# A fused attention, mixer and expert kernel: the mixer's normalisations on ScalarE, its first statistics in the attention loop, biases in the weights, ranks summed on TensorE, four pipeline stages in another order

## What is computed

```python
x = x + agent_attention(group_norm(x))          # masked attention over the 16 agents, 5 masks
t = x.reshape(32, 512, 128)
n = ln(t)                                       # (v - mean) / sqrt(var + 1e-5), per token
q, k, v = elu(n @ Wq + bq) + 1, elu(n @ Wk + bk) + 1, n @ Wv + bv      # 8 heads of 16
t = t + q @ (k.T @ v) / (q @ k.sum(tokens))     # linear attention, per sample and head
n = ln(t)
logits = n @ router_w + router_b                # 8 experts; the best two, softmax over the two
t = t + sum over the two experts of share * expert(n)
```

## Time and profile before

| | |
|---|---|
| median of 3 runs | 1396.28 us (1394.41 to 1402.51) |
| the profiled execution | 1391.66 us, span of its trace 1389.8 us |
| mean granted PE clock | 0.889 of 2.4 GHz |
| busy share of the span | PE 81%, DVE 70%, ACT 47%, POOL 41% |
| HBM | 33.47 MB read, 24.72 MB written, 42 GB/s over the span |

### The profile page before, as it was taken

How to read it: one execution, slowest core, us unless ns; L and a number is a source line. 1 busy time by engine, 2 the same in 40 slices (tenths; PEclk the granted TensorE clock), 3 DMA queues, 4 the chain that set the end, 5 groups by cost and what they waited for, 6 DMA issues and landing times. The chain is left out here.

```text
span 1389.8 us, 39348 instructions
## 1 busy us (share of the span) xinstructions
PE 1127.9 (81%) x12771; PEld 888.4 (64%) x12772; DVE 966.2 (70%) x2723; ACT 653.5 (47%) x1221; POOL 574.5 (41%) x575
## 2 busy tenths in 40 slices
PE   4599999999749978767777841099999999999995
PEld 4377877777615565546455541088888888887884
DVE  5476666766436887887878777077777777777774
ACT  0276665666214432232332310166666666666663
POOL 0335556555611133453354445234444444444443
PEclk9899999999959877777878765599999999999997
DMA  7010101010030001111111113911111111111100
GB/s 269 18 46 26 33 25 34 25 33 10 3 108 16 16 15 49 32 45 48 32 39 50 37 60 75 124 46 50 43 51 50 47 49 43 48 51 50 37 20 1
DMA packets 72632, 64.40 MB, mean 46 GB/s; under 512 B 10098, under 2 KB 58512, under 8 KB 72522
## 3 DMA queue, kind: packets, MB, share of 16 engines
q1 hardware_dynamic: 58698, 43.91, 11.5%
q0 software_dynamic: 10016, 17.16, 4.0%
q10 hardware_dynamic: 3808, 1.91, 1.1%
HBM read 33.47 MB, written 24.72 MB: 42 GB/s over the span
## 5 line engine op out<-in xcount | busy, mean ns | idle before, releaser
L1295 PE MATMUL e_ps<-e_xt,w_hl 128*128 128x256 f16 x736 | 202.1, 275 | 18.6 <-issue 16.0
L1247 POOL DMA_INDIRECT out<-e_y,e_xg x184 | 182.0, 989 | 78.9 <-issue 78.9
L1372 DVE SCALAR_TENSOR_TENSOR e_hid_hl<-e_hid,e_hid_hl 128x512 f16<-128x512 f32 x184 | 127.4, 693 | 108.7 <-ACT e_hid_hl L1345 96.1
L1296 PE MATMUL e_ps<-e_xt,w_hl 128*128 128x256 f16 x736 | 201.3, 274 | 0.0
L1297 PE MATMUL e_ps<-e_xt,w_hl 128*128 128x256 f16 x736 | 201.2, 273 | 0.0
L1345 ACT ACTIVATE e_hid_hl<-e_hid 128x512 f16<-128x512 f32 x184 | 115.9, 630 | 143.9 <-DVE e_hid L1366 82.3
L756 POOL TENSOR_TENSOR m_stw<-m_stw,m_half 128x8 f32<-128x8 f32 x32 | 53.6, 1682 | 263.8 <-DVE m_stw L1015 263.8
L1312 PE MATMUL e_ps<-w_hl,e_hid_hl 128*128 x736 | 153.9, 223 | 0.0
L1311 PE MATMUL e_ps<-w_hl,e_hid_hl 128*128 x736 | 152.5, 223 | 0.0
L768 POOL DMA_INDIRECT rows<-m_rows,m_place x128 | 130.9, 1023 | 50.4 <-issue 40.5
L1313 PE MATMUL e_ps<-w_hl,e_hid_hl 128*128 x736 | 151.4, 220 | 0.0
(11 more groups left out here) (241 smaller groups left out, 2759.9 us busy)
## 6 DMA issues: line engine op xcount, KB each, us to landing
e_xg<-rows SPq DMA_DIRECT2D x92, 133.0 KB
resid<-in_x SPq DMA_DIRECT2D x8, 1024.0 KB, 12.5
xb<-in_x SPq DMA_DIRECT2D x32, 256.0 KB, 2.6
m_rows<-resid SPq DMA_DIRECT2D x32, 256.0 KB, 2.7
out<-e_y,e_xg POOLq DMA_INDIRECT x184
m_w_f<-in_L_ffn_gate_up_proj SPq DMA_DIRECT2D x1, 2048.0 KB, 8.8
rows<-m_rows,m_place POOLq DMA_INDIRECT x128
rows<-nobody SPq DMA_DIRECT2D x15, 133.0 KB
```

The lines of the kernel that those rows point to most:

```text
L1247: nc.gpsimd.indirect_dma_start(out_rows, bass.IndirectOffsetOnAxis(ap=who, axis=0), y[:, slot, i, :], None, bounds_check=B * TOK - 1, oob_ ...
L1295: t.matmul(o, hi, x2[0], start=True, stop=False)
L1296: t.matmul(o, hi, x2[1], start=False, stop=False)
L1372: v.scalar_tensor_tensor(hid_hl[:, i, 1].rearrange("p q n -> p (q n)"), hid[:, i], 1.0 / (WS * QG), hid_hl[:, i, 0].rearrange("p q n -> p ...
```

## The change

- **Normalisations on ACT.** Both `norm` stages become 128x128 activations (Identity with scale and bias from a tile). POOL makes scale and bias: after the pow it also multiplies mean and factor, and adds the constant `lift`, all in the small tiles. The words rstd, shift and token number are written by ACT (`meta`).
- **First statistics in the attention loop.** The eight bn_stats per pair are DVE instructions of block 1 (`statistics`, one body behind `add`). In the mixer the six small instructions run once over all pairs, and POOL raises 8, then 16, then 104 columns.
- **Biases in the weights.** Wq, Wk, Wv and the router are one tile `wall`. (bias + 1 for q and k) is spread over the 128 rows of the weights and the mean of the columns taken out (`wall`, once), with LIFT making the transposed input carry the constant. So the bias matmuls, the bias operand of the exp, and the bias addition in `route` go. exp takes a bias of -1, and max(min(exp, 1), q) read from PSUM replaces relu and addition; the Relu passes go.
- **Ranks on PE.** The one-hot is f16; 18 small matmuls per pair add region base, earlier counts, earlier partitions and earlier tokens of the same partition. `sum16`, `same`, `earlier`, `spot` go from DVE. The ranks read a DVE result that stands after the whole of `route`.
- **Four bodies deep instead of six**, another order on every engine, `route` and statistics no longer woven. Folds go four experts per body in bodies 0 and 1; the weights' splits in three parts of 3, 3 and 2 experts, the last `weights_low` after the table.
- **Loads.** Constants, weights and biases of the mixer are loaded by SP at the end of the attention's second pass.

The diff, cut to its core ("..." marks what is left out):

```diff
@@ agent_attention
+            for tile, source in mixer["loads"]:
+                sp.dma_start(tile, source).then_inc(mixer["loads_in"], 16)
...
+            def statistics(k, ring, u):
+                e = 2 * k + u
+                ...
+                for j in range(TILES):
+                    v.bn_stats(mixer["st1"][:, e, j, :], resid[:, e, j * C:(j + 1) * C])
...
-                (3, add, 0), (1, reciprocals), (3, add, 1),
+                (4, statistics, 0), (4, statistics, 1), (3, add, 0), (1, reciprocals), (3, add, 1),
             ])
+            for u in range(2):
+                statistics(PAIRS - 1, 0, u)
@@ token_mixer, gpsimd
+            def power(k, ring):
+                w = stw[:, ring]
+                pool.wait_ge(s.stat2, LN_STEPS * (k + 1))
+                ...
+                g.tensor_tensor(w[:, 5, :], w[:, 4, :], half[:, 0:8], ALU.pow).then_inc(s.pow2, 1)
+                g.tensor_tensor(w[:, 6, :], w[:, 3, :], w[:, 5, :], ALU.mult).then_inc(s.pow2, 1)
+                g.tensor_tensor(w[:, 5:7, :], w[:, 5:7, :], ..., ALU.add).then_inc(s.pow2, 1)
...
+            pipelined(pool, PAIRS, 4, 2, [
+                (0, ring_power), (3, rows_ready), (3, send, 0), (3, send, 1), (0, biases_low), (1, power),
@@ token_mixer, scalar
+            def norm2(k, ring, u):
+                b = 2 * k + u
+                need(act, s.pow2, 3 * k + 3)
+                need(act, s.xT2, b - 1)
+                for j in range(TILES):
+                    i = u * TILES + j
+                    ins = a.activation(xn2[:, u, j * C:(j + 1) * C], resid[:, b, j * C:(j + 1) * C], ACT.Identity,
+                                       scale=stw[:, ring, 5, i:i + 1], bias=stw[:, ring, 6, i:i + 1])
+                ins.then_inc(s.norm2, 1)
...
+            pipelined(act, PAIRS, 4, 2, [
+                (0, norm1, 0), (2, norm2, 0), (0, xt_, 0), (0, norm1, 1), (0, queries, 0), (2, xt2_, 0), (2, norm2, 1), (0, xt_, 1),
+                (0, values, 0), (2, xt2_, 1), (0, keys, 0), (0, queries, 1), (2, meta), (0, keys, 1), (2, ew), (0, values, 1),
+                (0, weights), (0, biases),
@@ token_mixer, tensor
+            t.matmul(bank_s[:, 0:WALL], minus64[:], wall[:], start=True, stop=False)
+            t.matmul(bank_s[:, 0:WALL], plus64[:], wrow[:], start=False, stop=True).then_inc(s.wall_psum, 1)
...
-                    t.matmul(banks_kv[:, n], ones16[0:64, :], bkv_hl[:].rearrange("p i c -> p (i c)"), start=True, stop=False)
...
             def ranks(k, ring):
+                need(pe, s.route, ROUTE_STEPS * k + ROUTE_STEPS)
+                need(pe, s.place_done, k)
+                t.matmul(rank, part16[:], each(base16[:], 8), start=True, stop=False)
+                t.matmul(rank, ones16[:], each(ahead16[:], 8), start=False, stop=False)
+                for n in range(7):
+                    t.matmul(rank[:, (n + 1) * G:8 * G], ones16[:], each(oh16[:, n, :], 7 - n), start=False, stop=False)
+                t.matmul(rank, before16[:], oh16[:].rearrange("p n g -> p (n g)"), start=False, stop=True)
+                for n in range(8):
+                    last = t.matmul(seen, ident16[:], oh16[:, n, :], start=n == 0, stop=n == 7)
...
+            pipelined(pe, PAIRS, 4, 2, [
+                (1, sums, 0), (0, xT, 0), (1, outs, 0), (1, sums, 1), (0, q, 0), (2, xT2, 0), (1, outs, 1), (0, xT, 1), (0, k_v, 0),
+                (2, xT2, 1), (2, logits, 0), (2, logits, 1), (0, q, 1), (0, k_v, 1), (0, fold), (2, ranks),
@@ token_mixer, vector
+            small(chain(dve, s.stat1, 0), st1[:].rearrange("p b j n -> p (b j) n"), stw1[:])
+            v.scalar_tensor_tensor(wall[:], wall[:], 2.0, bank_s[:, 0:WALL], ALU.mult, ALU.add).then_inc(s.wall_done, 1)
...
+            def queries(k, ring, u):
+                ...
+                v.scalar_tensor_tensor(qf[:, u, :], ef[:, u, 0, :], 1.0, bank_q, ALU.min, ALU.max).then_inc(s.qf_done, 1)
...
             def keys_values(k, ring, u):
-                v.tensor_tensor(kv[:, u, 0:C], bank_s[:, 0:C], const(cst, "block_kv"), ALU.mult)
-                v.tensor_tensor(kv[:, u, C:C + H], bank_s[:, C:C + 1].to_broadcast([P, H]), const(cst, "block_ks"), ALU.mult).then_inc(s.kv_done, 1)
+                v.tensor_tensor(kv[:, u, :], bank_s[:, 0:C + H], const(cst, "block_kv"), ALU.mult).then_inc(s.kv_done, 1)
...
+            def placed(k, ring):
+                need(dve, s.rank_psum, k + 1)
+                step(v.tensor_tensor(picked[:], oh16[:], rank.rearrange("p (n g) -> p n g", g=G), ALU.mult))
+                step(v.tensor_reduce(best[:, 10, :], picked[:], AX.X, ALU.add))
+                step(v.tensor_copy(place[:, slot:slot + 2, :], w3(best[:, 10, :])), False)
+                v.tensor_tensor(ahead16[:], ahead16[:], seen, ALU.add).then_inc(s.place_done, 1)
...
+            pipelined(dve, PAIRS, 4, 2, [
+                (1, keys_values, 0), (1, mixed, 0), (1, keys_values, 1), (1, statistics, 0), (1, mixed, 1), (0, queries, 0), (1, statistics, 1),
+                (1, second_stats), (0, keys, 0), (2, route), (0, queries, 1), (2, shares), (2, placed), (0, keys, 1),
+                (0, folded), (0, weights_early),
```

More of the change, by code:

```diff
@@ L43 @@
 ROW = C + 5
[L44 removed]
+LN_STEPS, ROUTE_STEPS, EXP_STEP, PLACE_STEPS, COLUMN_STEP = 7, 14, 9, 10, 26
+WALL = 3 * C + E
 LIFT = 0.5
@@ L78, in _constants @@
     put(1, "region", np.tile(np.arange(G) * float(REGION), (P, 1)))
-    put(1, "earlier", np.tile((np.arange(8)[:, None] > np.arange(8)[None, :]).reshape(-1) * 1.0, (P, 1)))
+    put(1, "lift", np.concatenate([np.zeros((P, 8)), np.full((P, 8), LIFT)], 1))
     packed = np.array([E * a + b for a, b in PAIRS_OF] + [1])
@@ L927, in fold @@
                 pe.wait_ge(s.b_in, 32)
-                for e in range(2 * k, 2 * k + 2):
+                for e in range(4 * k, 4 * k + 4):
                     need(pe, s.fold_done, e)
@@ new lines, in statistics, with second_stats @@
+            def statistics(k, ring, u):
+                b = 2 * k + u
+                if isinstance(b, int):
+                    dve.wait_ge(s.add_done, b + 1)
+                for j in range(TILES):
+                    ins = v.bn_stats(st6[:, u * TILES + j, :], resid[:, b, j * C:(j + 1) * C])
+                if u:
+                    ins.then_inc(s.stat2, 1)
+            def second_stats(k, ring):
+                need(dve, s.stat2, LN_STEPS * k + 1)
+                need(dve, s.norm2, 2 * k - 2)
+                need(dve, s.meta_done, k - 1)
+                small(chain(dve, s.stat2, LN_STEPS * k + 1), st6[:], stw[:, ring])
@@ L1086, in route @@
-                pair = const(cst, "pair_code").rearrange("p (o g) -> p o g", o=1).to_broadcast([P, 8, G])
-                yield from step(v.tensor_tensor(oh[:], wide(best[:, 8, :], G), pair, ALU.is_equal), False)
-                other = best[:, 8:9, :].to_broadcast([P, 8, 8])
-                yield from step(v.tensor_tensor(same[:], wide(best[:, 8, :], 8), other, ALU.is_equal))
-                with nc.allow_low_precision(reason="counts up to 8"):
-                    counts = v.tensor_reduce(sum16[:], oh[:].rearrange("p n g -> p g n"), AX.X, ALU.add)
@@ L1092, in route @@
-                yield from step(counts, False)
-                yield from step(v.tensor_tensor(same[:], same[:], const(cst, "earlier").rearrange("p (n m) -> p n m", n=8), ALU.mult))
-                yield from step(v.tensor_reduce(best[:, 10, :], same[:], AX.X, ALU.add), False)
-            def placed(k, ring):
-                d, slot = 2 * k, 2 * ring
+                found3 = logit.rearrange("p (n e) -> p n e", e=E)
+                step(v.tensor_reduce(best[:, 0, :], found3, AX.X, ALU.max))
@@ L1125, in placed @@
-                need(dve, s.place_done, k + 1)
-            pipelined(dve, PAIRS, 6, 2, [
-                (2, keys_values, 0), (1, norm, 0, 0, xn, s.pow1, s.norm1), (4, norm, 0, 1, xn2, s.pow2, s.norm2),
-                (1, norm, 1, 0, xn, s.pow1, s.norm1), (4, norm, 1, 1, xn2, s.pow2, s.norm2), (2, keys_values, 1),
-                (2, mixed, 0), (3, mixed_ready), [(4, route), (0, stats, 0, s.stat1), (3, stats, 1, s.stat2)], (4, placed),
-                (1, feature, 0), (2, mixed, 1), (5, weights_low), (1, feature, 1), (0, folded),
+                step(v.tensor_tensor(rows[:, slot:slot + 2, :, WLO], w3(two), w3(more), ALU.add), False)
```

386 lines of the change are left out of this document (195 added, 191 removed).

## The result

The changed kernel took 1356.66 us (median of 4 runs, 1352.62 to 1364.09) against 1395.35 for the kernel before: a ratio of 0.9736, 95% interval 0.9695 to 0.9776. Faster, by 39 us; 1269 was forecast, and the range ended at 1312. The profiled execution took 1352.62 us, its span is 1350.8.

What follows compares the result with a forecast made beforehand. DVE's queue, the fullest, plus hand-offs bound the mixer. Early bodies to 481, twelve of 18.5 to 703, last place 731, plus 37: experts at 768 instead of 895.4, 127 less; 1264.5 profiled, 4.6 more for the median: 1269 us, range 1245 to 1312.

Steps and rivals of the forecast that it cites:

- idle time of the steady body: Mixer's looped body: DVE's loop turn 0.9, hand-offs 1.6 and low clock 0.5 us, added to 15.4 of work.
- `mixed` 1 meets `outs` 1: Steady mixer body: DVE reaches this product and waits some 0.4 us for PE's result.
- POOL 13, under cover: Steady mixer body: POOL's sends 10.4 us, one pow 1.65 and four tiny instructions sum to 13, fitting under 18.5.
- body 18.1: Steady mixer body: forecast about 18.5 us, from 15.4 + 0.9 + 1.6 + 0.5.
- DVE's work: Steady mixer body: DVE's remaining instructions sum to 15.4 us against 21.1 before.
- last place: End of the mixer: the last place known at 731 us instead of 857.1.
- tail: From the last place to the experts: 37 us, against 38.3 before, with the same bytes except one pair's leftovers.
- the mixer's first body: Start of the mixer: statistics, two key/value products at 1.2 GHz and four folds, ending body 0 at 416 us.
- 1: Mixer's PE clock stays at 0.80, giving 21.5 us a body and 1308 us; chance 0.17.
- 2: Mixer's ACT sets the pace, `norm2` waiting for POOL behind eight sends: body 21, 1302 us; chance 0.10.
- The rule of the page: Normalisations: multiply and add belong on VectorE; the move trades 4.2 us of its queue for 6.2 on ScalarE.
- 5: PE gets 1.2 GHz throughout the mixer, 31.6 us a body, about 1465 us, slower than before; chance 0.04.

Runs made afterwards that it cites:

- e12: Changed kernel with POOL's sends in two groups of four, second norm's power and next pair's lift between: 1315.3 us, 0.9421 of before.
- set C: Group of runs on one chip without late signals: the unedited changed kernel (1259.1 us, 0.9203 of before), and versions with split or paced sends.
- e2: Changed kernel with POOL's sends moved behind the power of the second norm: 1378.8 us, 27.3 us a body.
- e4: Changed kernel with the second norm's power between the first four and last four sends of a pair: 1299.0 us, 21.4 us a body.
- e7: Changed kernel without the mixer's sends and with no rows counted for the experts: 1259.9 us, 17.9 us a body; only the mixer is compared.
- e14: Changed kernel with SP sending the 532-byte rows to fixed places, POOL only signalling, no rows counted: 1267.0 us, 17.8 us a body.

## Why the prediction was wrong

**The step that failed** is the idle time of the steady body: 0.9 for a loop turn, 1.2 for `outs` 0, 0.4 for "`mixed` 1 meets `outs` 1", 0.5 for low clock, in all 3.0 us (3.1 by the rounded 18.5). Without late signals it measured 3.8 (18.1 less DVE's 14.3). With them it is 10.5: DVE waits 3.5 us for `outs` 1 each time instead of 0.4, ACT 4.9 for `xT` 1, PE then 4.3 for ACT's copy, and the clock falls from 0.97 to 0.83, while PE's work goes from 14.9 to 18.5 us. Of DVE's 6.7 us more, 2.8 are waits for `outs`; 1.5, 1.3 and 1.1 are waits for ACT's exponentials of the shares, ACT's keys and PE's logits, which stand behind the late `xT` 1 on PE and ACT. On the whole program the two kinds of run of the same kernel differ by 92.3 us (spans 1350.8 and 1258.5): 86.1 to the last `placed` (821.9 and 735.8), 6.1 in the experts.

**"POOL 13, under cover"** counted the sends as work on POOL's queue. That was right (busy 10.4 us a body, and 2.6 idle between the sends) and beside the point: what they cost is laid on PE's signals. The earlier trace rows mixed that cost with hand-offs, as 26.3 us a body at a clock of 0.80; the "remote" waits, 25.6 us in ten bodies, were the place to see it, and I took the time for ordinary idling that the new order would remove. The new order made it dearer. Before, five bodies in ten show such a wait at the one place and five at the other, 2.5 and 2.7 us on average; after, they come in ten and in all of eleven, at 3.5 and 4.9. My reading is that in the shorter body `outs` 1, `xT` 1 and the shared bank stand one behind the other right beside the sends; e12, where they don't, fits that, but moves other work too, so it isn't shown.

**What held**, in set C: body 18.1 (18.5 forecast); DVE's work 14.3 (15.4, some 1 too much); PE 14.9 (16); ACT 11.7 (12.4); POOL 10.3 and 2.6 between its sends (13 with them); last place at 735.8 (731); tail 35.0 (37); experts from 770.8 (768); the whole 1259.1 (1269), 7 us of the gap from experts that take 487.7 there instead of the 494.4 of before. Of the start the profile after shows: first attention statistics' end at 383.2, the mixer's first body over near 418 (416), the second at 448.5 (441, one fold at 1.2 GHz waits 4.2 us instead of 2.3), the next in 20.3 and 22.8 (20 each).

**The rivals.** 1 had the clock at 0.83 where it said 0.80, but as a result, not as a cause: in set C the same code gets 0.97. 2 named ACT waiting for POOL behind the sends; the waits show `norm2` waits for it once in set C, for 0.6 us, and never in the first trace. 2's mechanism does exist one queue further: e2 and e4 made ACT wait for the lift, at 9.5 and 4.0 us a body. 5, slower than before, is far off (its own terms make 1468 us, not 1465). The rule of the page "ScalarE: Activation LUTs" of the Trainium skill (section "Rules for kernel authors") against multiply and add on ScalarE did no harm here: the trace has ACT idle for 6.4 us of the 18.1 (set C). The case that happened, signals that come late whatever the order, was not on the list, and a bound for it could be had from the two rows of before: 2.5 us at each of two places in each of 13 bodies is 65 us, and with it the range would have ended at 1377.

## What to carry to other kernels

Read each wait that the profile can't put down to an instruction, add them up for the stretch that you mean to shorten, and ask what else ran just then; time that vanishes in no queue doesn't shrink with the queues. Before an experiment is read, its control has to be in the same set of runs: one edit looked like a gain of 100 us until the unedited kernel was measured beside it, and then it gave 15. Where sends from POOL can't be had another way, keep the signals that two engines hand to and fro away from them, and put small work that others wait for ahead of them on POOL's queue.

## What the runs showed of the hardware that I had not expected

- In three of five sets (and in the first profiles) PE's signals came up to 6 us after the modelled end of their matmuls in the stages where POOL's indirect DMAs run (mixer up to 6.0, experts up to 1.7); not in the mixer of e7 and e14, which has none of them, nor in the attention, which has one; in two sets never, with the same files, and once on the same chip. What differs between sets is open.
- It doesn't depend on how much is sent: 4 bytes a row 24.7 us a body, 532 bytes 24.9 to 25.3. The same bytes from SP: 17.8.
- The page "Perfetto Trace Analysis" of the Trainium skill (section "Tensor Engine Instruction (MATMUL, LD_WEIGHTS)") says that the end of a matmul is estimated and that its signal goes out only when PSUM has acknowledged all bytes. The trace agrees in that the two can part, by up to 6 us here; whether it is the acknowledgement or the way of the signal that is held, no run tells.
